# One operation in place of two for the rectified first layer of an expert, on ScalarE and on VectorE

## What is computed

```python
h = relu(x @ W1[e] + b1[e])      # 128 -> 256, for each of 8 experts
y = h @ W2[e] + b2[e]            # 256 -> 128
out = sum over the two best experts of  w[e] * y
```

## Time and profile before

| what | value |
|---|---|
| median of 3 runs | 1039.58 us (1037.6 to 1040.91) |
| profiled execution, first to last instruction (its span) | 1047.2 us |
| own time of the profiled execution | none is recorded beside its span |
| PE, PEld busy | 1001.0 us (96%), 570.0 us (54%) |
| DVE, ACT, POOL busy | 810.4 us (77%), 854.0 us (82%), 512.3 us (49%) |
| jobs 0 to 55 | about 14 to 196 us |
| first stream of tiles | about 350 to 442 us |
| second stream of tiles | about 783 to 886 us |
| jobs 56 to 103 | about 886 to 1040 us |

### The profile page before, as it was taken

The page is one execution under the profiler, slowest core; times in us unless marked ns, Lnnn a source line. Parts: engine busy times, 40 slices in busy tenths (PEclk is TensorE's granted clock), DMA queues, the critical chain, the costliest instruction groups (busy, mean ns, idle before and its releaser), DMA issues.

```text
span 1047.2 us, 20635 instructions
## 1 busy us (share of the span) xinstructions
PE 1001.0 (96%) x6665; PEld 570.0 (54%) x6665; DVE 810.4 (77%) x2226; ACT 854.0 (82%) x1240; POOL 512.3 (49%) x602
## 2 busy tenths in 40 slices
PE   7899999999999999999999999999999999999996
PEld 5677777533332588733222323323328887777774
DVE  6889999866767577667778777777638876999998
ACT  4655554699999999799999999999998997666653
POOL 5546777744445000046667666765321000687775
PEclk8999999999999999999999999999999999999999
DMA  6533223000060344211111111112513362344442
GB/s 191 182 122 132 102 102 102 14 20 20 19 179 27 91 141 148 105 41 29 36 37 34 36 36 34 37 34 63 145 56 122 123 241 91 122 136 137 147 157 81
DMA packets 58479, 96.20 MB, mean 92 GB/s; under 512 B 8595, under 2 KB 29467, under 8 KB 58371
## 3 DMA queue, kind: packets, MB, share of 16 engines
q1 hardware_dynamic: 47248, 73.63, 21.2%
q0 software_dynamic: 9728, 19.94, 6.6%
q10 hardware_dynamic: 1396, 1.30, 0.4%
HBM read 58.46 MB, written 36.39 MB: 91 GB/s over the span
## 4 chain that ended last, share of the span: by engine, by line
PE 57%; ACT 19%; DVE 11%; issue 10%; DMA 2%; SPq 0%; ACTq 0%; DVEq 0%; POOL 0%; POOLq 0%
ACT probs L1924 11%; PE ps L1698 9%; ACT sums L1924 6%; PE ps L1683 5%; DVE low L949 3%; PE ps L695 3%; PE ps L679 3%; PE ps L681 3%; PE ps L700 3%; PE ps L696 3%; PE ps L680 3%; PE ps L1316 2%; PE ps L1318 2%; PE ps L1327 2%; PE ps L1317 2%
## 5 line engine op out<-in xcount | busy, mean ns | idle before, releaser
L1924 ACT ACTIVATE probs<-ps 128x1024 f32<-128x1024 f32 x344 | 336.8, 1122 | 11.8 <-PE ps L1683 11.3
L1639 POOL DMA_INDIRECT found<-tiles,home x152 | 153.0, 1006 | 276.2 <-ACT sums L1924 122.2
L1627 POOL DMA_INDIRECT sorted<-xn,slot x152 | 153.3, 1008 | 125.7 <-ACT probs L1924 75.0
L1127 ACT ACTIVATE high<-ps 128x512 fp32r<-128x512 f32 x208 | 120.4, 594 | 82.3 <-PE ps L681 66.6
L1698 PE MATMUL ps<-probs,value 128*32 128x512 f32 x1376 | 183.2, 604 | 2.2 <-ACT probs L1924 1.6
L1924 ACT ACTIVATE sums<-ps 128x1024 f32<-128x1024 f32 x168 | 173.7, 1121 | 4.1 <-PE ps L1683 3.5
L1683 PE MATMUL ps<-shared 32*128 32x512 f16 x1024 | 143.0, 384 | 13.4 <-ACT probs L1924 5.6
L949 DVE SCALAR_TENSOR_TENSOR low<-ps,high 128x512 fp32r<-128x512 f32 x208 | 133.4, 682 | 15.0 <-ACT high L1127 13.5
L1203 POOL TENSOR_TENSOR sums<-sums 128x512 f32<-128x512 f32 x70 | 90.7, 1295 | 60.4 <-DVE sums L983 49.5
L1683 PEld LDWEIGHTS ps<-shared 32*128 32x128 f16 x1024 | 37.5, 91 | 143.5 <-ACT probs L1924 70.7
L695 PE MATMUL ps<-high,weights 128*128 128x512 f32 x208 | 84.4, 406 | 7.8 <-DVE sums L983 7.7
(11 more groups left out here) (202 smaller groups left out, 1878.5 us busy)
## 6 DMA issues: line engine op xcount, KB each, us to landing
probs<-gates SPq DMA_DIRECT2D x28, 512.0 KB
found<-sorted SPq DMA_DIRECT2D x52, 256.0 KB, 2.6
tiles<-sums SPq DMA_DIRECT2D x52, 256.0 KB, 2.0
wide<-gates SPq DMA_DIRECT2D x24, 512.0 KB
sorted<-zeros SPq DMA_DIRECT2D x16, 512.0 KB
out<-X SPq DMA_DIRECT2D x15, 256.0 KB
sorted<-xn,slot POOLq DMA_INDIRECT x152
found<-tiles,home POOLq DMA_INDIRECT x152
```

The costliest lines, as they stand in the source:

```text
L1127: nc.scalar.activation(high[:, third(m), c, :], ps[:, hidden_bank(m, c), :], ACT.Relu).then_inc(sm["f_high"], 1)
L1627: nc.gpsimd.indirect_dma_start(sorted_rows[group_of(q)], bass.IndirectOffsetOnAxis(ap=slot[:, q % XNS, k, j:j + 1], axis=0), xn[:, rows_sl ...
L1639: nc.gpsimd.indirect_dma_start(found[:, q % 2, k, j, :], None, tile_rows[group_of(q)], bass.IndirectOffsetOnAxis(ap=home[:, q, k, j:j + 1] ...
L1924: nc.scalar.activation(ring[ring_at(n)], ps[:, score_banks(n), :], ACT.Exp, scale=SCORE).then_inc(sm["a_probs"], 1)
```

## The change

The two operations of `relu` become one of 128 x 1024 over both halves (and both PSUM banks), which waits until both halves of hidden are there; likewise the two of `halve` and `ffn_halve`, which wait for the whole of `high`. `f_high`, `f_low`, `t_high` and `t_low` now count units, not halves. TensorE's waits follow: hidden of a unit waits for all of `low` two units before it ahead of its first matmul, and expert waits once for `high` and once for `low`. TensorE's matmuls and everybody's order stay as they are. The changes in the stream, with those in the jobs alike:

```diff
+        def tile_banks(t):
+            return slice(tile_bank(t, 0), tile_bank(t, 0) + C)
...
             for c in range(C):
                 at = slice(c * P, (c + 1) * P)
                 o = ps[:, tile_bank(t, c), :]
-                    reached(pe, sm["t_low"], (t - 2) * C + c + 1)
...
+                reached(pe, sm["t_low"], t - 1)
...
+                pe.wait_ge(sm["t_high"], t + 1)
                 for c in range(C):
-                    pe.wait_ge(sm["t_high"], t * C + c + 1)
...
+                pe.wait_ge(sm["t_low"], t + 1)
                 for c in range(C):
-                    pe.wait_ge(sm["t_low"], t * C + c + 1)
...
             def halve(t):
                 reached(dve, sm["t_expert"], t - 1)
-                for c in range(C):
-                    dve.wait_ge(sm["t_high"], t * C + c + 1)
-                    nc.vector.scalar_tensor_tensor(low[:, t % 2, c, :], ps[:, tile_bank(t, c), :], 0.0,
-                                                   high[:, t % 2, c, :].bitcast(F32), ALU.max, ALU.subtract).then_inc(sm["t_low"], 1)
+                dve.wait_ge(sm["t_high"], t + 1)
+                nc.vector.scalar_tensor_tensor(low[:, t % 2, :, :], ps[:, tile_banks(t), :], 0.0,
+                                               high[:, t % 2, :, :].bitcast(F32), ALU.max, ALU.subtract).then_inc(sm["t_low"], 1)
...
             def relu(t):
                 reached(act, sm["t_expert"], t - 1)
-                for c in range(C):
-                    act.wait_ge(sm["t_hidden"], t * C + c + 1)
-                    nc.scalar.activation(high[:, t % 2, c, :], ps[:, tile_bank(t, c), :], ACT.Relu).then_inc(sm["t_high"], 1)
+                act.wait_ge(sm["t_hidden"], (t + 1) * C)
+                nc.scalar.activation(high[:, t % 2, :, :], ps[:, tile_banks(t), :], ACT.Relu).then_inc(sm["t_high"], 1)
```

More of the change, by code:

```diff
@@ L346, in hidden_bank, with hidden_banks @@
             return 2 * (score_pair(m % 2) if m < WHOLE * E else tile_pair(1, 2 - m % 2)) + c
+        def tile_banks(t):
+            return slice(tile_bank(t, 0), tile_bank(t, 0) + C)
+        def hidden_banks(m):
+            return slice(hidden_bank(m, 0), hidden_bank(m, 0) + C)
         def output_bank(m):
@@ L671, in ffn_hidden @@
                 pe.wait_ge(sm["f_xl"], n + 1)
+            if m in (WHOLE * E, WHOLE * E + 1):
+                pe.wait_ge(sm["t_low"], TILE0[2] - 1 + m % 2)
+            else:
+                reached(pe, sm["f_low"], m - 1)
             for c in range(C):
@@ L674, in ffn_hidden @@
                 o = ps[:, hidden_bank(m, c), :]
-                if m in (WHOLE * E, WHOLE * E + 1):
-                    pe.wait_ge(sm["t_low"], (TILE0[2] - 2 + m % 2) * C + c + 1)
-                else:
-                    reached(pe, sm["f_low"], (m - 2) * C + c + 1)
                 nc.tensor.matmul(o, weights[:, e, 0, at], xh[:, u, :], start=True, stop=False)
@@ L691, in ffn_expert @@
                 pe.wait_ge(sm["w2_low"], m // PAIR + 1)
+            pe.wait_ge(sm["f_high"], m + 1)
             for c in range(C):
                 at = slice(c * P, (c + 1) * P)
-                pe.wait_ge(sm["f_high"], m * C + c + 1)
                 nc.tensor.matmul(o, weights[:, e, 2, at], high[:, third(m), c, :], start=(c == 0), stop=False)
                 nc.tensor.matmul(o, weights[:, e, 3, at], high[:, third(m), c, :], start=False, stop=False)
+            pe.wait_ge(sm["f_low"], m + 1)
             for c in range(C):
                 at = slice(c * P, (c + 1) * P)
-                pe.wait_ge(sm["f_low"], m * C + c + 1)
                 ins = nc.tensor.matmul(o, weights[:, e, 2, at], low[:, third(m), c, :], start=False, stop=(c == C - 1))
@@ L946, in ffn_halve @@
             reached(dve, sm["f_expert"], m - 2)
-            for c in range(C):
-                dve.wait_ge(sm["f_high"], m * C + c + 1)
-                nc.vector.scalar_tensor_tensor(low[:, third(m), c, :], ps[:, hidden_bank(m, c), :], 0.0,
-                                               high[:, third(m), c, :].bitcast(F32), ALU.max, ALU.subtract).then_inc(sm["f_low"], 1)
+            dve.wait_ge(sm["f_high"], m + 1)
+            nc.vector.scalar_tensor_tensor(low[:, third(m), :, :], ps[:, hidden_banks(m), :], 0.0,
+                                           high[:, third(m), :, :].bitcast(F32), ALU.max, ALU.subtract).then_inc(sm["f_low"], 1)
         def ffn_vector(dve, first, last):
@@ L1124, in relu @@
                 reached(act, sm["f_expert"], m - 2)
-                for c in range(C):
-                    act.wait_ge(sm["f_hidden"], m * C + c + 1)
-                    nc.scalar.activation(high[:, third(m), c, :], ps[:, hidden_bank(m, c), :], ACT.Relu).then_inc(sm["f_high"], 1)
+                act.wait_ge(sm["f_hidden"], (m + 1) * C)
+                nc.scalar.activation(high[:, third(m), :, :], ps[:, hidden_banks(m), :], ACT.Relu).then_inc(sm["f_high"], 1)
             if first == 0:
@@ L1309, in hidden @@
                 pe.wait_ge(sm["t_xl"], t + 1)
+                if t in (a, a + 1):
+                    pe.wait_ge(sm["a_probs"], (PAUSE if a == 0 else S * G) * UNITS - 1 + t - a)
+                reached(pe, sm["t_low"], t - 1)
                 for c in range(C):
@@ L1312, in hidden @@
                     o = ps[:, tile_bank(t, c), :]
-                    if t in (a, a + 1):
-                        pe.wait_ge(sm["a_probs"], (PAUSE if a == 0 else S * G) * UNITS - 1 + t - a)
-                    reached(pe, sm["t_low"], (t - 2) * C + c + 1)
                     nc.tensor.matmul(o, chosen[:, t % 3, 0, at], xh[:, u, :], start=True, stop=False)
@@ L1674, in attn_scores @@
             if n == PAUSE * UNITS:
-                pe.wait_ge(sm["t_low"], TILE0[1] * C)
+                pe.wait_ge(sm["t_low"], TILE0[1])
             if n == PAUSE * UNITS + 2:
```

## The result

The changed kernel takes 1054.77 us (median of 4 runs, 1051.73 to 1055.71) where the kernel before takes 1038.59 on the same chip (median of 4, 1036.63 to 1040.91). The ratio is 1.0161, with a 95% interval of 1.0144 to 1.0179: slower by 16.7 us.

What follows compares the result with a forecast made beforehand. It took TensorE to bound the streams, with ScalarE's loop close behind, and TensorE and VectorE to bound the jobs by turns. Streams +12.8 and jobs +5 made +17.8, from 1039.58 to 1057.4 us; range 1048 to 1067.

Steps and rivals of the forecast that it cites:

- Bounds, streams: Streams before the change: TensorE's work of 3.67 us per slot bounds; ScalarE's loop of `relu` and `choose` takes 3.46.
- The start of `relu`: Streams: the merged `relu` waits for half 1 and starts 1.76 us behind the tile's first hidden matmul.
- The duration of `relu`: Merged ScalarE operation over 1024 columns: taken as 1.05 us, with ends of 1.00 and 1.12.
- The sum of the loop: Streams: `relu` start, `relu`, gap, `choose`, gap make 3.97 us per tile in place of 3.67, binding from the fourth tile.
- The reading of rows 4: First stream's last slot before the change: `choose` starts 0.05 behind `relu`'s end, register work hidden; hidden waits for `choose`.
- the prediction's own two lines: Slots at 3.97 us: 22 in the first stream give +6.8 us, 22 of 24 in the second +6.0; together +12.8.
- ScalarE's register work: Streams: the read of the expert's number runs beside `relu` for some 0.78 us, hidden behind 1.05; otherwise 0.13 more.
- the rival on it: Streams: register work not hidden, 0.13 to 0.18 us more per slot, +7 over 44 slots, 1064 us in all; chance 0.13.
- The jobs: Later `low` costs 0.5 us in each of eight to ten busy VectorE stretches; +5 taken, ends -3 and +9.
- The step on job 58: Jobs: job 58's hidden needs `low` of job 56, which ends later, so it waits 0.8 us.
- TensorE gets `scale` late by that: Jobs: VectorE, caught up, starts its next stretch up to 1.1 us late; `scale` is that late, less 0.07 per job.
- VectorE's saving: Jobs: the merged VectorE operation saves 0.07 us each, 7 over 104 jobs, of which about 1.4 counts inside the stretches.

Runs made afterwards that it cites:

- choose_first: The changed kernel with `choose` put ahead of the merged `relu` in ScalarE's order; 1056.68 us, ratio 1.0076 to the kernel before.
- first_before: The kernel before, halves kept, with `choose` put ahead of `relu` on ScalarE; 1051.19 us, ratio 1.0002 to the kernel before.
- act_only: The kernel before with only ScalarE's operation merged, in jobs and tiles, VectorE's halves each waiting for all of `high`; 1061.23 us, ratio 1.0156.
- streams_only: The changed kernel with the jobs put back to halves, so merged in the tiles alone; 1056.36 us, ratio 1.0061 to the kernel before.
- jobs_only: The changed kernel with the tiles put back to halves, so merged in the jobs alone; 1057.99 us, ratio 1.0072 to the kernel before.
- before_again: The kernel before under another name, without an edit, for a second profile on another chip; 1050.3 us, ratio 1.000.
- after_again: The changed kernel once more, without an edit, on a third chip; 1062.09 us, ratio 1.0153 to the kernel before.
- vector_where_bound: The kernel before with only VectorE's operation merged, in jobs 44 to 54, 70 to 90 and 94 to 98; 1051.15 us, ratio 1.0003.
- dve_only: The kernel before with only VectorE's operation merged, in jobs and tiles, ScalarE's halves kept; 1050.69 us, ratio 1.0043.

## Why the prediction was right, point by point

**Bounds, streams.** Right: ScalarE's loop with 0.2 in hand. choose_first and first_before show both sides of it: with `choose` out of the way the merged form costs an ordinary slot nothing, and with halves the swap brings nothing.

**The start of `relu`.** Forecast at H + 1.76, H being the start of the tile's first matmul; measured 1.76, in act_only 1.75.

**The duration of `relu`.** Taken as 1.05, measured 1028 ns in the streams. The estimate of 1.00 by the Trainium skill ("VectorE: DVE Perf Modes", TRN2 errata) is near; the trace gives 0.03 more and decides. (The exponential of the same size, also from PSUM, takes 1.12.)

**The sum of the loop: the step that was mis-sized.** "1.76 + 1.05 + 0.05 + 1.06 + 0.05 = 3.97" put the start of `choose` 0.05 behind the recorded end of `relu`, as in the earlier trace rows. It starts 0.10 before that end, 0.92 to 0.93 behind the start of `relu`. The reading of rows 4 that failed is that the register work is hidden there, and that the gap of 0.05 is ScalarE's own. The work starts with the last operation of `relu` and takes 0.64 from there at the least, which is longer than a half of 0.60. In the slot of rows 4 its last step starts at 437.7, 0.1 ahead of `choose`:

```profile
L1579 ACTq TENSOR_LOAD <-expert_of x1: 283/283/283, 437.2 to 437.2; - x1
L1581 ACTq FUSED_REGOPS  x1: 46/46/46, 437.7 to 437.7; - x1
```

Behind a single operation of 1.03 the same work has time. A slot of the changed kernel where its last step is over 0.3 before `choose`, so that only ScalarE itself can hold `choose` up:

```profile
386.62 1.03 ACT L1595 ACTIVATE high<-ps 128x1024 fp32r<-128x1024 f32 x1 [0.75 <-PE ps L1322]
387.55 1.05 ACT L1584 ACTIVATE chosen<-weights 128x1024 fp32r x1
...
L1584 ACTq FUSED_REGOPS  x1: 46/46/46, 387.2 to 387.2; - x1
```

There too `choose` starts 0.10 before the end of `relu`. So the period became 3.79 and not 3.97.

What that did to the sum: with 3.79 in them, the prediction's own two lines give 2.9 and 2.0 us, 4.9 in place of 12.8. The slots that they cover lost 3.2 and 2.8. Another 0.6 and 0.8 were lost in the step from each stream's second tile to its third, which the prediction left out because it took the loop to bind only from the fourth tile on. Together these are the 7.4 of the stages (6.4 by streams_only's ratio).

**ScalarE's register work.** In the changed kernel hidden, as forecast, and the rival on it fell: in 45 of the 48 slots of the first profile in which `choose` stands behind `relu` it starts some 0.10 before the recorded end of `relu`. But it is close. The read takes 0.27 to 0.65 us there, and in two slots the work ends late; `choose` then starts 0.17 and 0.28 behind `relu`, and the slots take 4.1 us.

**The jobs.** Forecast +5, measured +7.6 by jobs_only (5.9 to 9.2), inside the stated ends. (The terms that the prediction names for it, 4 to 5 for the stretches and 0.8 for job 58 less 1.4 of savings, make about 4; the +5 was chosen.) This too small term and the too large one for the streams cancelled. That the time came out within 3 us is therefore luck: the streams were forecast 5.4 us too dear. The mechanism of the streams is shown, the jobs' amount was a guess inside wide ends. The step on job 58 was right: 0.8 forecast, 0.86 measured. The step "TensorE gets `scale` late by that" named too narrow a waiter. The wait for `scale` rose from 15.2 to 18.5 us in the first pair of profiles, but not in the second (16.0 in before_again, 15.8 in after_again). TensorE also waits for `low` itself (3.6 us in the changed kernel and 1.8 in after_again, where before_again had 0.6) and for `gate` (1.5 and 2.5, where before_again had 0.4). The waits of the changed kernel, to be held against the earlier trace rows:

```profile
DVE low L954 <- ACT high L1131: 32.0, 38, 2.8
...
PEld ps L701 <- DVE sums L988: 18.5, 23, 2.9
...
PEld ps L685 <- DVE low L954: 3.6, 3, 1.3
...
PEld ps L653 <- DVE gate L906: 1.5, 1, 1.5
```

VectorE waits 12 to 18.5 us longer for `high`, and the jobs cost some 6 to 9 us in time; the remainder is absorbed where VectorE had time. Its earliest `low` came at H + 2.66, not 2.9.

**VectorE's saving.** 0.07 per unit was taken; 1.29 became 1.22, as said. It counted less than the 1.4 granted: vector_where_bound, which takes the saving where it should be free, gains nothing measurable.

**What was seen differently from the forecast signs.** PE idle until `choose` in some 40 slots was expected; the trace notes it 4 times, 2.0 us on PEld. In the other slots the 0.12 to 0.16 isn't shown as an idle time at all, and only the distance of two first matmuls shows it. For the same reason, and as the slot is only 3.8 long, PE's share of the stretch from 360 to 435 us is 99% and not 92%. In the second stream of after_again one slot (tile 41) is 1.2 longer for another reason, a DMA that brings a tile's rows. SyncE took 3.13 us to issue a copy of gates ahead of it (0.3 or 0.4 in the slots around it), and TensorE stood for the rows:

```profile
841.69 3.13 SPq L466 DMA_DIRECT2D wide<-gates  x1
...
847.37 0.66 PE L1306 MATMUL ps<-K,found 128*128 128x128 f32 x4 [1.03 <-DMA found<-sorted]
```

dve_only and jobs_only wait for it too (0.63 and 0.46), without so long an issue; it is missing in the first profile of the changed kernel, and what makes it come or go wasn't tried. The 2 to 3 us by which the change costs more than the sum of its two parts need no cause of their own, since the intervals allow them.

**Grouping.** The Trainium skill's rule on grouping ("Perfetto Trace Analysis", Optimizing Scalar/DVE Operations) says that larger operations can improve throughput if the engine is saturated. Here the engines had less to do (29 and 12 us less busy), and the time rose, since neither was held by its amount of work alone. The other rule of that section, which the prediction took for this case, asks for engines that aren't saturated; ScalarE fits that, since it stood for TensorE 37.5 us in front of the merged `relu` of the tiles.

## What to carry to other kernels

Merging two halves into one operation saves a start (0.07 us here on VectorE). In return it starts later by the time between the halves (0.70 us here on ScalarE), and nobody gets the first half before the whole is done. Before doing it, take the loop through one slot and compare it with the bounding engine's own work: here a loop longer by 0.33, with 0.21 in reserve, cost 0.12 to 0.16 in each of some 40 slots. If the merge is wanted all the same, move what is queued behind it and doesn't need it (here the copy of the weights) ahead of it.

A stop seen at TensorE may be caused several units earlier, by a wait of an engine that has no reserve until the stop. Follow the queue of the engine that it waits for back to its last idle time rather than change what stands at the stop. And before a gain of some tenths of a microsecond at one place is pursued, look whether two executions of the same code differ there by as much: here they differed by 0.7.

## What the runs showed of the hardware

- ScalarE starts its next operation before the recorded end of the one ahead: `choose` 0.10 before the end of a 1.03 `relu`, and in choose_first `relu` 0.09 before the end of a 1.06 `choose`. A period worked out from recorded ends is too long by that for each such step. Where register work stands between two operations, the second can start later: 0.05 and 0.18 behind the recorded end of a 0.60 half.
- The merged ScalarE operation over two PSUM banks takes 1028 ns where a pair without a wait takes 1.08; VectorE's takes 1218 to 1224 ns where the pair takes 1.29.
- Chips of the same kind differ by 1.2% in this kernel (1038.6 to 1051.1 us for before), and it shows mostly in one stage of exponentials and matmuls, not in the first stream, which took 86.4 us for before on two of them and 90.1 to 90.2 with the merged form on three.
- The granted clock was 0.50 and 0.51 between 30 and 36 us in two executions and 0.75 in the mean in a third, among kernels with and without merged jobs. It was 0.50 to 0.52 at jobs 92 and 93 in three more, behind a TensorE wait of 1.8 us that other executions have without a fall.
